# The first three steps of a second attention, moved into the tail of the dense programs before it

## The chip, the cores and the metric

The kernel runs on one NeuronCore of a Trainium2 chip. A core has five instruction queues that run side by side and meet only at semaphores: PE (matrix products, written to PSUM), ACT (ScalarE, functions of one tile), DVE (VectorE, elementwise work and sums), POOL (GpSimd) and SP (which starts DMAs). PSUM has eight banks of 512 float32 for each of 128 partitions; SBUF is the working memory. The metric is the device time of one execution in microseconds (us), the median of several runs.

## What is computed

Four blocks follow each other on a tensor x of 16 sequences x 256 tokens x 128 channels, each added to its input and normalised:

```python
x = layernorm(x + L0_attention(x))   # bucketed attention and a dense MLP
x = layernorm(x + L0_ffn(x))         # 8 experts on every token, gates from a global k-th value
x = layernorm(x + L1_attention(x))   # 4 local heads (softmax), 12 causal linear heads
x = layernorm(x + L1_ffn(x))         # 8 experts, top 2 of each token
```

The third line is the second attention. For each sequence (a block of 256 tokens) it needs x turned (channels on partitions), projections to q, k and v, a softmax over a causal window of 128 for four heads, and for the twelve others softmaxed queries against running sums of keys and values.

## The kernel before

The program has three stages, each with its own instruction block: `attention_0`, `dense_0` and `attention_1` (which also holds the routed experts at its end). Between two blocks every engine waits for every other, and the semaphores of the stage are cleared. Each stage allocates its own PSUM banks and SBUF tiles and gives them back.

`dense_0` runs 72 jobs (`JOBS`): 8 chunks of 512 tokens through the MLP, then 64 pairs of chunk and expert. A job is four hidden products into the banks `HB` (line 1097 to 1099), a gelu and a rounded copy on ACT (890, 895), a rest on DVE (936), and a down product into one of two banks `YB`. DVE then folds YB into the sum of the chunk (993, 1004): a down product waits until the fold of two jobs before has read its YB bank. `hidden` runs two jobs ahead (`LEAD`), so that the last two jobs issue down products alone and ACT has nothing left to do. When the last pair of a chunk is folded, PE turns the sum into the bank `PB` (1129), DVE adds the residual (`r`, 1055), takes mean and variance (1059, 1063), POOL raises the variance to -1/2 (876, 877), and DVE writes the normalised chunk to `keep["xa"]` (1085). Chunks end in the order 3, 0, 4, 5, 1, 6, 2, 7: chunk 2 at step `CLOSING` (69), chunk 7 at step 73, where the loop is otherwise empty. Up to 22 pairs are kept raw until the gates are known, 16 of them in `x1` and `xs`, the places of the first attention's results; the last of these 16 is folded at step 58.

`attention_1` works on 16 blocks of 256 tokens in a pipeline written out by hand. `PARTS_1` lists, for each step, which part of which block every engine issues; `parts_1` walks steps 0 to 16 and then `DRAIN_1`. Every engine walks the same list and issues only what is its own. The parts that matter here: `lift` (PE turns x into `BA`, 2124; ACT copies it to `xT`, 1874), `project` (PE, 2128, 2129; ACT rounds into `high`, 1879, 1880), `bias` (POOL adds a bias to x in place, 1822), `low` (DVE, 1958), `wide` (PE, 2134, into `BC` and `BD`), `heads` (DVE, 1966, 1971), `features` (ACT, 1896 to 1904, with the exponential), `keys` and `queries` (DVE, 1977, 1984, 1985), `scores` (PE into `SS`, 2156 to 2161), `max` (DVE, 1989, 1990), `context` (PE, 2144 to 2147; DVE divides, 2011 to 2015), `pad`, `qT`, `shift`. Step 0 has lift 0 alone; step 1 the projections and features of block 0 and lift 1; step 2 scores, max and context of block 0, projections and features of block 1, and lift 2. `wide` of a block waits for the division of the block before it, which reads the bank it overwrites.

`fetch` and `split` carry the routed experts' weights: SP brings a share of each matrix in, ACT scales it and rounds it (1935, 1938), POOL forms the rest (1827). Share n comes in step n + 1, two places in a ring. Before its steps, POOL of `attention_1` clears tiles (1801 to 1814).

The step list, cut to what is quoted above:

```python
PARTS_1 = [
    [("scores", 2), ("max", 2), ("project", 1), ("context", 2), ("pad", 2), ("back", 4), ("qT", 2), ("fetch", 1), ("bias", 1)],
    [("weights", 3), ("offset", 5), ("low", 1), ("wide", 1), ("heads", 1), ("shift", 2), ...
     ("features", 1)],
    [("values", 3), ("linear", 3), ("keys", 1), ("queries", 1), ("lift", 0), ("copy", 3), ... ("split", 1)]]
```

## Time and profile before

| | us |
|---|---|
| median of 3 runs | 1030.87 |
| their range | 1030.49 to 1030.97 |
| the profiled execution | 1030.6 |
| its span, first to last instruction | 1028.9 |
| PE busy | 933.9 (91%) |
| DVE busy | 817.0 (79%) |
| ACT busy | 780.1 (76%) |
| POOL busy | 433.2 (42%) |

The span is what lies between the first and the last recorded instruction; 1.7 us of the profiled execution lie around it. A busy time counts an engine's instructions, not its waits. A share of 91% over the whole span says little of a stage of 30 us, so that the stage is read by itself below. The granted clock (PEclk) is 1.00 at 2.4 GHz and 0.50 at 1.2 GHz.

### The profile page before, as it was taken

How to read it: one execution, taken by the hardware profiler on the slowest of the kernel's cores; microseconds unless marked ns; L12 is line 12 of the kernel's file. 1: busy time of each engine (PE TensorE's matmuls, PEld its weight loads, DVE VectorE, ACT ScalarE, POOL GpSimd, SP SyncE). 2: the span in 40 equal slices, each digit the busy share in tenths (PEclk: the TensorE clock that was granted, in tenths of full speed). 3: DMA queues.
4: the chain of work that ended last, by engine and by line, in shares of the span. 5: the costliest groups of instructions: out<-in, count | busy, mean ns of one | idle time of the engine just before them, and what ended most of it. 6: DMA issues, size and time to landing. Idle time of an engine off the chain costs nothing. (4 is left out here: it accounts for less than half of the span.)

```text
span 1028.9 us, 29035 instructions
## 1 busy us (share of the span) xinstructions
PE 933.9 (91%) x10222; PEld 603.1 (59%) x10222; DVE 817.0 (79%) x2282; ACT 780.1 (76%) x1537; POOL 433.2 (42%) x613
## 2 busy tenths in 40 slices
PE   5999999988999999999999999488888865899995
PEld 3788888874555444444444444256565644789862
DVE  4898888853777999688899899578888867888845
ACT  3789998977998888888888788166776643788844
POOL 3667777762352000000100100224687777666653
PEclk9999999987999999999999999789999975999998
DMA  8433333101000000222123221110111103232327
GB/s 273 146 127 126 130 128 127 46 23 33 1 1 1 1 1 1 77 83 80 55 81 88 67 82 52 34 32 22 41 57 49 49 25 82 78 87 82 82 59 213
DMA packets 61005, 72.60 MB, mean 71 GB/s; under 512 B 8875, under 2 KB 37805, under 8 KB 60865
## 3 DMA queue, kind: packets, MB, share of 16 engines
q1 hardware_dynamic: 50080, 59.36, 18.9%
q0 software_dynamic: 4544, 8.60, 2.5%
q10 hardware_dynamic: 6240, 2.79, 1.1%
q8 instruction: 86, 1.41, 0.6%
q14 instruction: 55, 0.44, 0.1%
HBM read 40.14 MB, written 31.49 MB: 70 GB/s over the span
## 5 line engine op out<-in xcount | busy, mean ns | idle before, releaser
L890 ACT ACTIVATE d__hf<-d__HB,dense__d 128x512 f32<-128x512 f32 x288 | 185.6, 680 | 48.4 <-PE d__HB L1099 47.4
L936 DVE TENSOR_TENSOR d__hl<-d__hf,d__hh 128x1024 f16<-128x1024 f32 x144 | 174.2, 1220 | 28.3 <-ACT d__hh L895 26.0
L876 POOL TENSOR_SCALAR d__rstd<-d__mv 128x4 f32<-128x4 f32 x16 | 14.2, 887 | 338.1 <-DVE d__mv L1063 338.1
L895 ACT ACTIVATE d__hh<-d__hf 128x1024 f16<-128x1024 f32 x144 | 152.2, 1057 | 4.6
L1097 PE MATMUL d__HB<-dense__xh,dense__w1h 128*128 128x512 f16 x288 | 110.0, 382 | 2.8 <-ACT d__hf L890 1.5
L1097 PE MATMUL d__YB<-d__hh,dense__w2h 128*128 128x512 f16 x288 | 109.2, 379 | 2.5 <-DVE d__tmp L993 2.5
L1098 PE MATMUL d__HB<-dense__xl,dense__w1h 128*128 128x512 f16 x288 | 110.1, 382 | 0.0
L1099 PE MATMUL d__HB<-dense__xh,dense__w1l 128*128 128x512 f16 x288 | 109.9, 382 | 0.0
L1098 PE MATMUL d__YB<-d__hl,dense__w2h 128*128 128x512 f16 x288 | 109.2, 379 | 0.0
L1099 PE MATMUL d__YB<-d__hh,dense__w2l 128*128 128x512 f16 x288 | 109.2, 379 | 0.0
L370 POOL TENSOR_SCALAR_AFFINE_SELECT a__pt<-a__pt 128x512 f32<-128x512 f32 x128 | 83.7, 676 | 56.6 <-ACT a__pt L418 56.6
L508 DVE TENSOR_REDUCE a__mx<-a__S 128x4 f32<-128x512 f32 x128 | 82.0, 683 | 20.6 <-PE a__S L612 20.4
L1358 POOL DMA_INDIRECT parts<-c__ys,c__dest x78 | 81.3, 1042 | 39.5 <-issue 17.6
L418 ACT ACTIVATE a__pt<-a__ST 128x512 f32<-128x512 f32 x128 | 69.4, 596 | 13.2 <-PE a__ST L628 13.1
L1844 POOL DMA_INDIRECT rows<-b__xr,b__slot x64 | 63.5, 992 | 21.5 <-issue 17.0
L1376 ACT ACTIVATE c__hf<-b__SS,c__bias 128x256 f32<-128x256 f32 x156 | 61.1, 474 | 7.5 <-PE b__SS L1585 6.8
L1512 DVE TENSOR_TENSOR c__hl<-c__hf,c__hh 128x512 f16<-128x512 f32 x78 | 54.2, 695 | 2.7
L1097 PEld LDWEIGHTS d__HB<-dense__xh,dense__w1h 128*128 128x128 f16 x288 | 30.4, 105 | 35.2 <-ACT d__hf L890 3.0
L1097 PEld LDWEIGHTS d__YB<-d__hh,dense__w2h 128*128 128x128 f16 x288 | 28.2, 98 | 36.0 <-DVE d__tmp L993 4.5
L1099 PEld LDWEIGHTS d__HB<-dense__xh,dense__w1l 128*128 128x128 f16 x288 | 28.3, 98 | 34.7 <-issue 1.1
L1099 PEld LDWEIGHTS d__YB<-d__hh,dense__w2l 128*128 128x128 f16 x288 | 28.2, 98 | 34.0
L1098 PEld LDWEIGHTS d__YB<-d__hl,dense__w2h 128*128 128x128 f16 x288 | 28.2, 98 | 31.8
(413 smaller groups left out, 2547.3 us busy)
## 6 DMA issues: line engine op xcount, KB each, us to landing
rows<-a__blank SPq DMA_DIRECT2D x72, 268.0 KB, 3.0
d__G<-gates SPq DMA_DIRECT2D x64, 256.0 KB, 3.2
c__xin<-rows SPq DMA_DIRECT2D x39, 134.0 KB, 2.2
dense__stage<-e_w SPq DMA_DIRECT2D x16, 256.0 KB, 3.2
b__stage<-e_w SPq DMA_DIRECT2D x32, 128.0 KB, 2.3
c__yb<-parts SPq DMA_DIRECT2D x8, 256.0 KB, 8.1
c__yb<-parts ACTq DMA_DIRECT2D x8, 256.0 KB, 8.8
out<-c__xo SPq DMA_DIRECT2D x8, 256.0 KB, 2.5
```

The source lines that it names most:

```text
L370: pool.affine_select(out=v, in_=v, compare_op=ALU.is_ge, fill=0.0, base=BK, pattern=[[0, 8], [1, BK]], channel_multiplier=-1).then_inc(cau ...
L418: act.activation(pt[:, u % 4, :], ST[:, u % 2, :], ACT.Exp, scale=scale).then_inc(exp_done, 1)
L508: dve.tensor_reduce(mx[:, u // 4, :, u % 4], S[:, u % 2, :].rearrange("p (a j) -> p a j", a=4), AX.X, ALU.max).then_inc(s_free, 1)
L890: act.activation(hf[:, q, f], HB[:, f], gelu, scale=1.0 / WS, bias=b1[:, at:at + 1]).then_inc(s_["h_free"], 1)
L895: act.activation(hh[:, j % (LEAD + 1), f - 1:f + 1], hf[:, q, f - 1:f + 1], ACT.Copy).then_inc(s_["hi_done"], 1)
L936: dve.tensor_tensor(hl[:, p, f], hf[:, q, f], hh[:, p, f], ALU.subtract).then_inc(s_["lo%d_done" % i], 1)
L1097: pe.matmul(dst, wh, vh, start=begin, stop=False)
L1098: pe.matmul(dst, wh, vl, start=False, stop=False)
L1099: return pe.matmul(dst, wl, vh, start=False, stop=end)
L1358: pool.indirect_dma_start(parts, bass.IndirectOffsetOnAxis(dest[b % RING][:, a:a + 1], 0), ys[b % RING][:, a, :], None, bounds_check=2 * T ...
L1376: ins = act.activation(hf[b % 2][:, f], HB[:, b % 2, f // 2, f % 2], ACT.Gelu, scale=1.0 / WS, bias=bias[:, f, b:b + 1])
L1844: pool.indirect_dma_start(rows, bass.IndirectOffsetOnAxis(slot[n % SENT][:, k, a:a + 1], 0), words[n % SENT][:, a, :], None, bounds_check= ...
```

## The change

The first three steps of `attention_1` (`EARLY_1`, 25 parts: lift 0, then block 0's projections and features, then block 0's scores and context and block 1's projections and features, up to lift 2) are issued from inside `dense_0`'s block. To make that possible the eight PSUM banks become one tensor `keep["banks"]` that both stages cut up (the attention's `BA` to `BD` are the banks of `HB`, its `SS` those of `YB`, `PB` and `QB`), and the attention's tiles come from `keep["lease"]`, the place of `x1` and `xs`. `attention_1` becomes a generator: it first hands out its early parts, and after the dense block it goes on with `MAIN_1`.

Where the early parts stand in each queue: PE issues lift 0 after the down product of the last job but one, project 0 and wide 0 after the last one, lift 1 after the last chunk is turned, and the rest (from scores 0) once the last read of PB is done. DVE issues low 0 and heads 0 at step `CLOSING` after the last folds and ahead of the normalised write of chunk 2; keys 0 and queries 0 between the variance of chunk 7 and its normalised write; the rest after that. ACT goes through its early parts after its loop, behind a first exponential on a scrap tile. POOL clears the tiles at step 66, after the raw pairs are folded, and adds the biases of blocks 0 and 1 after its last rstd. `fetch` and `split` stay behind: shares 0 and 1 both come in step 3, 2 and 3 both in step 4, then one in each step as before. The dense loop ends one empty step earlier.

```diff
+                if s == CLOSING - 3:
+                    pool.wait_ge(s_["g_used"], place[LAST_RAW] + 1)
+                    second["clears"](pool)
...
+            pool.wait_ge(keep["att_in"], 16 * 5)
+            in_order(EARLY_1, second["gpsimd"](pool))
...
+            act.wait_ge(keep["att_in"], 16 * 5)
+            second["warm"](act)
+            in_order(EARLY_1, second["scalar"](act))
...
                 if s == CLOSING:
                     fold(s + 1)
                     fold(s + 2)
+                    dve.wait_ge(keep["att_in"], 16 * 5)
+                    in_order(EARLY_1[:OPEN_1], attention)
...
+                if s == END - 1:
+                    in_order(EARLY_1[OPEN_1:LOOK_1], attention)
                 if post:
                     c = post[1]
...
+            in_order(EARLY_1[LOOK_1:], attention)
...
                 if 0 <= s < JOBS:
                     down(s)
+                if s == JOBS - 2:
+                    pe.wait_ge(s_["h_free"], 4 * JOBS)
+                    pe.wait_ge(keep["att_in"], 16 * 5)
+                    in_order(EARLY_1[:1], attention)
+                if s == JOBS - 1:
+                    in_order(EARLY_1[1:OPEN_1], attention)
...
+            in_order(EARLY_1[OPEN_1:LOOK_1], attention)
+            for q in range(2):
+                pe.wait_ge(s_["yf%d" % q], JOBS // 2)
+            pe.wait_ge(s_["pb_free"], len(left))
+            in_order(EARLY_1[LOOK_1:], attention)
...
+EARLY_STEPS = 3
+SPLITS_1 = {EARLY_STEPS: (0, 1), EARLY_STEPS + 1: (2, 3)}
...
+EARLY_1 = [u for s in range(EARLY_STEPS) for u in steps_1(s)]
+MAIN_1 = [u for s in range(EARLY_STEPS, NB + 1) for u in steps_1(s)] + DRAIN_1
+
+OPEN_1 = EARLY_1.index(("heads", 0)) + 1
+LOOK_1 = EARLY_1.index(("lift", 1)) + 1
...
+        def warmed(act):
+            act.wait_ge(s["cleared"], CLEARED_VALUES)
+            act.activation(scrap[:], half[:], ACT.Exp).then_inc(s["warm"], 1)
```

## Rows read from the trace of the kernel before

**Rows 1.** Chain that ended last, 660 to 690 us: start, length, engine, tile, line
```profile
...
666.00 1.28 ACT L1902
...
673.21 1.44 PE b__BC L2134 x2
...
681.89 0.81 PE b__BC L2134 x2
...
```

**Rows 2.** Busy time of single microseconds: engines (PE first), PEclk, DMA share, GB/s
```profile
...
652.00:653.00 1.00, 0.56 (x4) 0.32 (x4) 0.93 (x4) 0.00 (x0) 0.00 (x0) 0.80 0.00 0
...
666.00:667.00 1.00, 0.43 (x3) 0.01 (x1) 0.00 (x0) 1.00 (x1) 0.00 (x0) 0.88 0.00 0
...
676.00:677.00 1.00, 1.00 (x14) 0.45 (x12) 0.79 (x5) 0.44 (x4) 0.00 (x0) 0.76 0.00 0
...
```

**Rows 3.** Timeline of the dense tail: start, length, engine, line, tile, idle before and releaser
```profile
...
645.75 0.39 PE L1097 MATMUL d__YB<-d__hh,dense__w2h 128*128 128x512 f16 x1 [1.13 <-DVE d__tmp L993]
...
651.82 1.11 DVE L1085 TENSOR_SCALAR keep__xa<-d__r,d__mv,d__rstd 128x128 f32<-128x128 f32 x4
...
651.93 0.63 PE L1129 MATMUL d__PB<-keep__ident,d__acc 128*128 128x128 f32 x4 [3.42 <-DVE d__acc L1004]
653.04 0.69 DVE L1055 TENSOR_TENSOR d__r<-d__PB,keep__xa 128x512 f32<-128x512 f32 x1
...
656.67 1.11 DVE L1085 TENSOR_SCALAR keep__xa<-d__r,d__mv,d__rstd 128x128 f32<-128x128 f32 x4 [1.51 <-POOL d__rstd L877]
...
```

**Rows 4.** Timeline of the second attention's first steps, same columns
```profile
...
659.24 0.66 PE L2124 MATMUL b__BA<-keep__ident,keep__xa 128*128 128x128 f32 x2 [6.68 <-PEq L100]
...
660.00 0.38 ACT L1874 ACTIVATE b__xT<-b__BA 128x256 f32<-128x256 f32 x1 [19.28 <-PE b__BA L2124]
...
660.44 1.22 PE L2128 MATMUL b__BA<-b__xT,keep__b 128*128 128x256 f32 x2 [0.54 <-ACT b__xT L1874]
...
662.31 1.27 PE L2134 MATMUL b__BC<-keep__b,b__xT 128*128 128x320 f32 x2
...
663.41 0.48 DVE L1958 SCALAR_TENSOR_TENSOR b__qs<-b__high,keep__b,b__BA 128x256 f16<-128x256 f16 x1 [5.62 <-ACT b__high L1880]
...
665.01 0.41 PE L2156 MATMUL b__SS<-b__ks,b__qs 32*128 32x256 f16 x4
...
665.46 0.98 PE L2161 MATMUL b__SS<-keep__bbf 128*128 128x256 bf16 x4
...
669.78 0.64 PE L2144 MATMUL b__BC<-b__gv,b__kf 64*96 64x97 f32 x2
...
671.99 0.16 DVE L2011 TENSOR_SCALAR b__den<-b__BC 96x3 f32<-96x3 f32 x1 [1.16 <-PE b__BC L2147]
...
675.75 0.26 DVE L1966 TENSOR_REDUCE b__qm<-b__BC 128x12 f32<-128x96 f32 x1 [1.51 <-PE b__BD L2134]
...
678.32 0.70 PE L2128 MATMUL b__BA<-b__xT,keep__b 128*128 128x256 f32 x2 [1.07 <-ACT b__xT L1874]
...
678.71 1.16 DVE L1989 TENSOR_REDUCE b__mx<-b__SS 128x4 f32<-128x1024 f32 x1
...
680.67 0.16 DVE L2011 TENSOR_SCALAR b__den<-b__BC 96x3 f32<-96x3 f32 x1 [0.20 <-PE b__BC L2147]
...
683.27 0.26 DVE L1966 TENSOR_REDUCE b__qm<-b__BC 128x12 f32<-128x96 f32 x1 [0.35 <-PE b__BD L2134]
...
```

**Rows 5.** Timeline of POOL, then DVE, at one place of the dense programs
```profile
...
314.65 1.15 POOL L871 TENSOR_TENSOR dense__xl<-d__xT,dense__xh 128x512 f16<-128x512 f32 x1
...
314.71 1.94 DVE L1085 TENSOR_SCALAR keep__xa<-d__r,d__mv,d__rstd 128x128 f32<-128x128 f32 x4 [0.80 <-POOL d__rstd L877]
...
```

**Rows 6.** Timeline of ScalarE where step 3 passes into step 4
```profile
...
685.89 0.69 ACT L1935 ACTIVATE b__stage<-b__stage 128x512 f32<-128x512 f32 x1
...
688.12 0.38 ACT L1879 ACTIVATE b__high<-b__BA 128x256 f16<-128x256 f32 x1 [0.79 <-PE b__BA L2129]
...
689.89 0.38 ACT L1884 ACTIVATE b__qT<-b__BD 96x256 f32<-96x256 f32 x1 [1.02 <-PE b__BD L2140]
...
```

More of the change, by code:

```diff
@@ L1674, in blocks_1, with attention_1 @@
     return early, sync, gpsimd, scalar, vector, tensor, scalar_early, vector_early, tensor_early
-def attention_1(nc, d, keep, rows, parts, out, w1, w2, whole):
+def attention_1(nc, d, keep, rows, parts, out, w1, w2, whole, weights):
     with ExitStack() as ctx:
@@ new lines, in attention_1 @@
+        den = lease.sb([GW, 3])
+        rinv = lease.sb([GW, 3])
+        ctxn = [lease.sb([GW, 4, GW]) for p in range(2)]
+        mx = lease.sb([P, 2, LH])
+        mpad = lease.sb([P, 2, LH, 32], F16)
+        q2 = lease.sb([P, 2, P], F16)
+        pt = lease.sb([P, LH, 3 * P])
+        ots = lease.sb([P, 2 * P])
+        rc = lease.sb([P, 2, LH])
+        ob = lease.sb([P, 2, C])
+        aT = lease.sb([P, TB])
+        half = lease.sb([P, 2])
+        r = lease.sb([P, 2, C])
+        st = lease.sb([P, 2, 6])
@@ L1755, in attention_1 @@
+        mv = lease.sb([P, 2, 2])
+        rstd = lease.sb([P, 2])
+        mean_off = lease.sb([P, 2])
+        x3T = lease.sb([P, TB])
+        SS = banks[:, 4:8]
+        BA, BB, BC, BD = (banks[:, i] for i in range(4))
         OT, LN = SS[:, 0, 0:2 * P], SS[:, 1, 0:2 * GW]
@@ L1766, in attention_1 @@
         s = {n: m.sem(n) for n in names.split()}
-        for p in range(SENT):
-            s["sent%d" % p] = m.sem("sent%d" % p)
+        s.update((n, None) for n in later.split())
         def row_free(eng, q):
             wait(eng, s["sent%d" % (q % SENT)], q // SENT * 128)
-        keep["ident16"] = ident16
-        (early, sync, gpsimd, scalar, vector, tensor, scalar_early, vector_early,
-         tensor_early) = blocks_1(nc, Mem(nc, ctx, "c", whole), d, keep, rows, parts, out, (SS, BA, BB, BC, BD), s)
         scale = float(HD) ** -0.5
@@ L2245, in step @@
                     ins.then_inc(s["join_full"], 1)
-            parts_1(step)
+            return step
+        yield {"clears": clears, "warm": warmed, "gpsimd": gpsimd_steps, "scalar": scalar_steps,
+               "vector": vector_steps, "tensor": tensor_steps}
+        weights()
+        for n in later.split():
+            s[n] = m.sem(n)
+        for p in range(SENT):
+            s["sent%d" % p] = m.sem("sent%d" % p)
+        G = keep["G"]
+        lg = m.sb("lg", [P, 4, E])
+        lm = m.sb("lm", [P, 4])
@@ new lines, in attention_1 @@
+        slot = [m.sb(f"slot{p}", [P, 2, 4], U32) for p in range(SENT)]
+        words = [m.sb(f"xr{p}", [P, 4, ROW]) for p in range(SENT)]
+        xr = [v[:].rearrange("p a c -> p (a c)").bitcast(F16).rearrange("p (a c) -> p a c", a=4) for v in words]
+        tok, kval, earlier, ones = f32["tok"], f32["kval"], bf16["earlier"], bf16["ones"]
+        base = keep["base"]
+        share = w1.shape[1] // NB
+        stage = m.sb("stage", [P, 2, 2, share])
+        split_to = ((w1, keep["w1h"], keep["w1l"]), (w2, keep["w2h"], keep["w2l"]))
@@ new lines, in attention_1, with share_of @@
+        parts_of = share // P
+        def share_of(w, n):
+            e, f = n * parts_of // FB, n * parts_of % FB
+            return w[:, f:f + parts_of, e * P:(e + 1) * P]
+        keep["ident16"] = ident16
+        (early, sync, gpsimd, scalar, vector, tensor, scalar_early, vector_early,
+         tensor_early) = blocks_1(nc, Mem(nc, ctx, "c", whole), d, keep, rows, parts, out, (SS, BA, BB, BC, BD), s)
+        hooks.update(scalar=scalar_early, vector=vector_early, tensor=tensor_early)
+        block = ctx.enter_context(nc.Block())
@@ new lines, in _, with step @@
+        @block.sync
+        def _(sp):
+            early(sp)
+            def step(what, n):
+                if what == "fetch":
+                    wait(sp, s["split_low"], n - 1)
+                    for a, (src, _, _) in enumerate(split_to):
+                        sp.dma_start(stage[:, n % 2, a],
+                                     src[:, n * share:(n + 1) * share]).then_inc(s["landed%d" % (n % 2)], 16)
+            in_order(MAIN_1, step)
+            sync(sp)
+        @block.gpsimd
@@ new lines, in _ @@
+        def _(pool):
+            for w in words:
+                pool.memset(w[:, :, C + 5], 0.0)
+            pool.memset(chosen[:, 4], 0.0).then_inc(s["cleared"], 1)
+            pool.wait_ge(s["cleared"], CLEARED_ALL)
+            in_order(MAIN_1, gpsimd_steps(pool))
+            gpsimd(pool)
+        @block.scalar
+        def _(act):
+            in_order(MAIN_1, scalar_steps(act))
+            scalar(act)
+        @block.vector
+        def _(dve):
+            in_order(MAIN_1, vector_steps(dve))
+            vector(dve)
@@ L2269, in program, with routed_weights @@
         keep["fetch_att"] = fetch_att
+        c2 = ctx.enter_context(ExitStack())
+        def routed_weights():
+            m2 = Mem(nc, c2, "routed", m)
+            for n in ("w1h", "w1l", "w2h", "w2l"):
+                keep[n] = m2.sb(n, [P, FB, E * P], F16)
+            keep["G"] = m2.sb("G", [P, NT, E])
+        second = attention_1(nc, d, keep, rows, parts, out, d["e1_w1"], d["e1_w2"], m, routed_weights)
+        early = next(second)
         with ExitStack() as c1:
```

251 lines of the change are left out of this document (109 added, 142 removed).

## The prediction

> **What bounds the kernel now.** I read the page's 40 slices first. PE is busy nine tenths nearly everywhere, but at the border between the dense programs and the second attention all engines thin out and PEclk falls. So the next views were the timeline of that border, the chain that ended last, and the busy time of single microseconds.
>
> The tail of the dense programs is a chain on DVE. PE's last down product is over 3.42 us before PE turns the last sum at 651.93; in that time DVE folds the last pairs, then it writes chunk 2, takes the statistics of chunk 7 (653.04), waits 1.51 us for POOL's rstd and writes chunk 7 until 657.78 [rows 3]. PE and ACT have next to nothing to do there: PE also stands 1.13 us before the last down product [rows 3], and ACT idles 19.28 us before the attention's first copy [rows 4].
>
> Then the barrier between the blocks: PE's first transpose starts at 659.24, 1.46 us after the last write [rows 3, 4]. From there the chain runs hand to hand. Block 0 has no other block beside it: turn, copy, project, round, wide, heads, features (with an exponential table load of 1.28 us in the chain), context, divide, wide of block 1, and so on [rows 1, 4]. PE runs most of it at 1.2 GHz: the clock drops in the microsecond 652, after PE has stood for most of the 3.42 us, comes back only in 666, has gone again by the time PE does wide 1, and is back for good in 676 [rows 2]. The same wide product takes 2.54 us at 1.2 GHz (673.21 to 675.75, where DVE begins to read) and 1.38 us at 2.4 GHz (681.89 to 683.27) [rows 1, 4]. I take as the mark of comparison the division of block 1's context on DVE at 680.67 [rows 4]: from there on each part is the same work in both kernels, and the chain continues to the end, so a shift at this mark is a shift of the end. From the end of the dense write (657.78) to this mark the old kernel takes 22.89 us.
>
> **The change, part by part.**
>
> Beside the tail, at no cost. Lift 0 takes 0.66 us even at 1.2 GHz [rows 4] and lies in PE's 1.13 us gap. Project 0 and wide 0 come after the last down product: 1.87 us (660.44 to 662.31) and 2.54 us at 1.2 GHz, 4.41 together [rows 1, 4]; at 2.4 GHz, which PE has there, I estimate half of the first and 1.38 of the second, 2.3. They begin near 648.5 and are over near 650.8, inside the 3.42 us. If that cover fails they end at 652.9, the last sum is turned 1 us later, and DVE, which by then has other work until 655.0, still does not wait. The table load and the clears stand in queues that are empty (ACT's 19.28 us; POOL waits for the last rstd), so that features 0 no longer contain the 1.28 us. Were the load still in the way, it would cost at most that. The clears write SBUF beside dense steps in which PE sets the pace: nothing, or some tenths on a DVE that has room.
>
> On the path, delaying the dense tail. DVE is a queue in order: low 0 (two instructions of 0.48) and heads 0 (four of 0.26) stand ahead of chunk 2's write, with chunk 7's statistics, POOL's rstd and chunk 7's write queued behind: 2.00 us [rows 4]. Keys 0 and queries 0 are four instructions of about 0.3 us and lie in the 1.51 us of waiting for rstd: nothing, at worst their own 1.2 us in part. The bias of blocks 0 and 1 on POOL now starts when rstd is done, just when DVE writes chunk 7. The nearest row is a place where a POOL tensor_tensor ran beside the same DVE write: 1.94 us in place of 1.11 [rows 3, 5]. I take these 0.83 us once; the bounds are nothing and twice that. The Trainium skill ("SBUF — State Buffer", section "Who interferes with whom") says that DVE and GpSimd share a port pair as an exclusive lock, and that the loser waits for the whole instruction; the row agrees. Without this the forecast would be 0.83 lower.
>
> After the dense write, until the early steps end. Max 0 takes 1.76 us (678.71 to 680.67 less 0.20 of waiting), and its scores are ready, as PE needs only DVE's last read of PB, some 4 us earlier. The division until wide can start takes 1.22 (680.67 to 681.89). Wide 1 takes 1.38 or 2.54; I take 1.38, since scores 0, project 1 and context 0 keep PE at work just before. From DVE's first read of wide 1 to the end of queries 1 it is 2.96 (675.75 to 678.71) [rows 1, 4].
>
> The barrier, now here: 1.46 us again, as the same block ends and the same semaphores are cleared. It also empties the pipeline. In the old kernel scores 1 and project 2 ran beside step 2's end; now PE issues them after the barrier, with context 1 behind, before the mark is reached: at 1.2 GHz scores 1.43 (665.01 to 666.44), project 1.87, context 2.21 (669.78 to 671.99), together 5.51. At 2.4 GHz project and context take 2.35 (678.32 to 680.67), and with an estimated half for scores 3.07 [rows 4]. Before the barrier PE stands for some 3 us while DVE finishes, and it stood about as long before the drop in 652 [rows 2, 3], so I take 5.51. The Trainium skill ("TensorE: Matmul & The Clock Gate", section "HAM oscillation — how this bites in real kernels") says that a wait between bursts makes PE start cold each time; the trace agrees (1.2 GHz after each of its two waits here), and this rule speaks against the change, which puts a wait there. If the clock held, the time would be 2.44 lower.
>
> The doubled splits. Two shares less in steps 1 and 2, where ACT waited anyway; one more in each of steps 3 and 4, 1.44 us on ACT (685.89 to 687.33). Behind it stands the rounding for the next block, before which ACT idles 0.79 us, and then qT, before which it idles 1.02 [rows 6]: 1.81 us of cover against 1.44, so nothing. If the first gap alone counts, it is 0.65 in each step, 1.30 in all. The fetches go out earlier than ACT needs them by the length of a step.
>
> Sum from 657.78: 2.00 + 0.83 + 1.76 + 1.22 + 1.38 + 2.96 + 1.46 + 5.51 = 17.12, so the mark is reached at 674.90 in place of 680.67: 5.77 us earlier. The profiled execution (1030.6, of which 1028.9 are span) becomes 1024.8; the median of the runs lies 0.27 above the profiled execution, so I forecast 1025.1.
>
> **The rivals.**
>
> The clock holds over the barrier. PE then refills in 3.07, and with no collision on the ports the gain is 5.77 + 2.44 + 0.83 = 9.04: 1021.8. For it: PE has more to do than in the old tail. Against: the trace shows the drop after a wait of this size [rows 2, 3].
>
> Half of the gain is lost. Wide 1 at 1.2 GHz (1.16), the second bias (0.83) and the splits on the path (1.30) together take 3.29: gain 2.48, 1028.4. Each of the three has a row that allows it, but they are not bound to come together.
>
> No change. The moved steps don't run where they are put: DVE waits in low 0 or heads 0 for PE or ACT, and the tail waits behind it. Each microsecond of that wait is one of the end; 5.8 us are needed, so heads 0 would have to start near 658.5 in place of 652.8. Against: the inputs are ready by 651 by the sum above. 1030.9.
>
> Slower: the clock stays at 1.2 GHz beyond the refill. Each further step in the cold costs 1.16 for wide, 1.73 for project and context (4.08 against 2.35) and about 0.7 for scores, 3.6 us [rows 1, 4]. It decides from the second such step on: two cost 7.2 against the 5.77 won, 1032.3. For it: the old kernel lost the clock twice in these steps. Against: both times it came back within some 7 us of PE's resuming [rows 2, 4], and the fourth step has more for PE than the second.
>
> **How the numbers follow.** The forecast has 0.55 (its own range 1023.5 to 1026.7), the held clock 0.14, the half gain 0.16, no change 0.09, slower 0.06. The range from 1021.8 to 1028.4 leaves out the last two and the outer edges of the others. A difference under 0.2%, 2 us, can hardly be told from no change by a measurement of this kernel. Faster by more: 0.55 + 0.14 + 0.16 = 0.85; same 0.09; slower 0.06.
>
> **What would show it.** Right: lift 0 before the last down product; the table load near 641; low 0 at 651.8 and chunk 2's write at 653.8; chunk 7's write ending near 660.6, its instructions stretched beside the bias; no 1.28 us load inside features 0; the barrier over near 669.4; PEclk 0.50 in scores 1 and project 2; the division of block 1's context near 674.9, and each later step earlier by the same amount. Wrong: DVE idle ahead of low 0 or heads 0; a gap in front of max 0; a refill at 2.4 GHz; ACT's split as the releaser of the rounding's readers; or an end that moves by another amount than the mark, which would mean that a later stage gives back or adds.

## The result and the profile after

The kernel after the change takes 1023.55 us (median of 4 runs, 1022.05 to 1024.88); the kernel before, on the same chip, 1030.68 (1030.41 to 1030.97). The ratio is 0.993, with a 95% interval of 0.9913 to 0.9948. The profiled execution of after took 1024.88, of which 1023.2 are span; that of before 1030.6 and 1028.9. So the gain is 7.1 us by the medians and 5.7 between the two profiled executions.

Three moments carry all that follows. **Fold's end** is the end of the last fold in the dense tail on DVE (651.78 before: the sum that PE turns at 651.93 [rows 3]). **Division 1** is the mark of the prediction, the division of block 1's context on DVE. **Keys 2** is DVE's reciprocal for block 2, a later mark that also serves for kernels which move more or less than this one. Distances from the fold's end can be compared between executions; absolute times cannot, as the run called "again" below shows.

The timeline of after, ACT around 641, then PE and DVE from lift 0 on (start, length, engine, line, operation, tile out<-in; in brackets the idle time before and what ended it):

```profile
641.61 1.28 ACT L1832 ACT_TABLE_LOAD   x1
...
645.48 0.38 PE L2132 MATMUL keep__banks<-keep__ident,keep__xa 128*128 128x128 f32 x2
...
646.77 0.39 PE L1131 MATMUL keep__banks<-d__hh,dense__w2h 128*128 128x512 f16 x1 [0.91 <-DVE d__tmp L1022]
...
650.24 1.24 PE L2142 MATMUL keep__banks<-keep__b,keep__lease 128*128 128x320 f32 x4
...
652.12 0.69 DVE L1033 TENSOR_TENSOR d__acc<-d__acc,d__tmp 128x512 f32<-128x512 f32 x1
652.85 0.87 DVE L1969 SCALAR_TENSOR_TENSOR keep__lease<-keep__lease,keep__b,keep__banks 128x256 f16<-128x256 f16 x2
652.96 0.63 PE L1163 MATMUL keep__banks<-keep__ident,d__acc 128*128 128x128 f32 x4 [1.48 <-DVE d__acc L1033]
...
654.42 1.10 DVE L1118 TENSOR_SCALAR keep__xa<-d__r,d__mv,d__rstd 128x128 f32<-128x128 f32 x4
...
656.58 0.41 PE L2164 MATMUL keep__banks<-keep__lease 32*128 32x256 f16 x4 [2.37 <-DVE d__r L1084]
```

Here the covered part of the move is to be seen. The table load stands at 641.61, lift 0 just ahead of the last down product, and wide 0 is over by 651.5 beside the folds. Before, these steps began at 659.24, and scores 0 behind them only at 665.01 [rows 4]. Low 0 stands right behind the last fold, at 652.85, and chunk 2's write follows at 654.42.

The same timeline further on, POOL, DVE and PE up to division 1:

```profile
659.20 1.68 POOL L1839 TENSOR_TENSOR keep__xa<-keep__xa,keep__bo 128x128 f32<-128x128 f32 x4
659.26 1.70 DVE L1118 TENSOR_SCALAR keep__xa<-d__r,d__mv,d__rstd 128x128 f32<-128x128 f32 x4 [0.61 <-POOL d__rstd L900]
...
662.62 0.14 DVE L2022 TENSOR_SCALAR keep__lease<-keep__banks 96x3 f32<-96x3 f32 x1
...
663.82 2.50 PE L2142 MATMUL keep__banks<-keep__b,keep__lease 128*128 128x320 f32 x4 [2.37 <-DVE keep__lease L2026]
...
666.36 0.42 DVE L1977 TENSOR_REDUCE keep__lease<-keep__banks 128x12 f32<-128x96 f32 x2 [1.51 <-PE keep__banks L2142]
...
669.10 0.30 DVE L1996 RECIPROCAL keep__lease<-keep__lease 128x24 f32<-128x24 f32 x1
670.85 0.41 PE L2164 MATMUL keep__banks<-keep__lease 32*128 32x256 f16 x4 [3.89 <-PEq L100]
...
675.15 0.16 DVE L2022 TENSOR_SCALAR keep__lease<-keep__banks 96x3 f32<-96x3 f32 x1 [0.96 <-PE keep__banks L2155]
```

And the busy time of single microseconds of after (PE first; PEclk is the first figure behind the engines' brackets, then DMA share and GB/s):

```profile
658.00:659.00 1.00, 1.00 (x4) 0.82 (x3) 0.62 (x3) 0.00 (x0) 0.92 (x2) 0.50 0.00 0
...
662.00:663.00 1.00, 0.00 (x0) 0.00 (x0) 0.94 (x4) 0.00 (x0) 0.00 (x0) 1.00 0.00 0
...
664.00:665.00 1.00, 1.00 (x2) 0.66 (x3) 0.85 (x3) 0.00 (x0) 0.00 (x0) 0.50 0.00 0
...
671.00:672.00 1.00, 1.00 (x12) 0.52 (x5) 0.00 (x0) 0.00 (x0) 0.91 (x4) 0.50 0.11 25
...
674.00:675.00 1.00, 1.00 (x8) 0.76 (x8) 0.19 (x1) 0.72 (x2) 0.00 (x0) 1.00 0.67 194
```

The clock falls three times between 656 and 674, each time in a wait of PE or at its end (waits of 2.37, 2.37 and 3.89 us, ahead of 656.58, 663.82 and 670.85), and comes back each time after some 3 us of work. Wide 1 lies in the second low (2.50 us). So the stage that the change shortened is still one in which PE runs much of its work at 1.2 GHz.

From the fold's end (652.81) to division 1 (675.15) it is 22.34 us; before it was 28.89 (651.78 to 680.67 [rows 4]). That is 6.55 won. The next divisions stand at 683.79, 692.77 and 702.70, against 689.30, 697.98 and 707.91: 5.51, 5.21 and 5.21 us earlier, hardly less than the 5.52 at the mark. The fold's end itself came 1.03 later, so that 5.5 are left of the 6.55; 0.2 more come out in the rest of the kernel, and 5.7 is the difference of the spans.

The 1.03 have two parts. POOL's rstd for chunk 6 comes 0.73 later (621.49 against 620.76); 0.67 of it is there already 38 us after the start, and it lies within what executions of one kernel differ by (see "again"). The rest, 0.30, is new, and lies in the dense tail itself:

```profile
623.53 0.81 POOL L1819 MEMSET keep__lease<- 128x256 f32 x3
623.58 1.41 DVE L1118 TENSOR_SCALAR keep__xa<-d__r,d__mv,d__rstd 128x128 f32<-128x128 f32 x4 [1.18 <-POOL d__rstd L900]
...
624.78 0.92 POOL L1827 MEMSET keep__lease<- 96x384 f32 x2
624.91 0.68 DVE L1019 TENSOR_TENSOR d__tmp<-dense__stage,d__G 128x512 f32<-128x512 f32 x1
```

These are POOL and DVE of after at chunk 6's normalised write: it takes 1.41 us beside POOL's clears. In the kernel before the same write stood alone:

```profile
622.85 1.11 DVE L1085 TENSOR_SCALAR keep__xa<-d__r,d__mv,d__rstd 128x128 f32<-128x128 f32 x4 [1.18 <-POOL d__rstd L877]
```

### The profile page after: what moved, and what is told of

It reads as the page before. It is cut to its first block and busy times, and to the rows that moved or that the text cites. A ratio compares the mean times of both kernels' runs of the same rounds, so it can differ in the third digit from the quotient of the medians.

```text
span 1023.2 us, 29039 instructions
## 1 busy us (share of the span) xinstructions
PE 932.2 (91%) x10222; PEld 602.8 (59%) x10222; DVE 818.4 (80%) x2282; ACT 779.9 (76%) x1538; POOL 433.3 (42%) x613
## 3 DMA queue, kind: packets, MB, share of 16 engines
q8 instruction: 86, 1.41, 0.6%
## 5 line engine op out<-in xcount | busy, mean ns | idle before, releaser
L915 ACT ACTIVATE d__hf<-keep__banks,dense__d 128x512 f32<-128x512 f32 x288 | 185.5, 680 | 48.5 <-PE keep__banks L1133 47.5
L1131 PE MATMUL keep__banks<-dense__xh,dense__w1h 128*128 128x512 f16 x288 | 110.1, 382 | 2.8 <-ACT d__hf L915 1.5
L1131 PE MATMUL keep__banks<-d__hh,dense__w2h 128*128 128x512 f16 x288 | 109.2, 379 | 2.4 <-DVE d__tmp L1022 2.4
L1132 PE MATMUL keep__banks<-dense__xl,dense__w1h 128*128 128x512 f16 x288 | 110.0, 382 | 0.0
L1133 PE MATMUL keep__banks<-dense__xh,dense__w1l 128*128 128x512 f16 x288 | 109.9, 382 | 0.0
L1132 PE MATMUL keep__banks<-d__hl,dense__w2h 128*128 128x512 f16 x288 | 109.2, 379 | 0.0
L1133 PE MATMUL keep__banks<-d__hh,dense__w2l 128*128 128x512 f16 x288 | 109.2, 379 | 0.0
L528 DVE TENSOR_REDUCE a__mx<-keep__banks 128x4 f32<-128x512 f32 x128 | 82.0, 682 | 20.8 <-PE keep__banks L632 20.5
L438 ACT ACTIVATE a__pt<-keep__banks 128x512 f32<-128x512 f32 x128 | 69.4, 596 | 13.2 <-PE keep__banks L648 13.1
L1440 ACT ACTIVATE c__hf<-keep__banks,c__bias 128x256 f32<-128x256 f32 x156 | 61.1, 474 | 7.5 <-PE keep__banks L1649 6.5
```

The costliest lines, as they stand in the source:

```text
L528: dve.tensor_reduce(mx[:, u // 4, :, u % 4], S[:, u % 2, :].rearrange("p (a j) -> p a j", a=4), AX.X, ALU.max).then_inc(s_free, 1)
L915: act.activation(hf[:, q, f], HB[:, f], gelu, scale=1.0 / WS, bias=b1[:, at:at + 1]).then_inc(s_["h_free"], 1)
L1131: pe.matmul(dst, wh, vh, start=begin, stop=False)
L1132: pe.matmul(dst, wh, vl, start=False, stop=False)
L1133: return pe.matmul(dst, wl, vh, start=False, stop=end)
```

## The experiments

Each run is compared by distances from its own fold's end. "Rest of the span" is the span less the time of the fold's end, all that comes after it. The ratio is to the kernel before, timed beside each run; the experiments come from three chips, so medians of different rows compare best through their ratios.

| kernel | division 1 | keys 2 | rest of the span | median us | ratio, 95% interval |
|---|---|---|---|---|---|
| before | 28.89 | 34.23 | 377.1 | 1030.68 | |
| after | 22.34 | 27.69 | 370.4 | 1023.55 | 0.9930 [0.9913, 0.9948] |
| again | 22.56 | 27.91 | 370.4 | 1023.95 | 0.9950 [0.9934, 0.9966] |
| late_bias | 21.78 | 27.13 | 370.2 | 1022.71 | 0.9938 [0.9917, 0.9958] |
| no_warm | 22.41 | 27.76 | 369.9 | 1023.45 | 0.9937 [0.9906, 0.9968] |
| two_steps | 25.09 | 31.74 | 373.6 | 1026.53 | 0.9961 [0.9944, 0.9979] |
| filled | 19.89 | 25.24 | 368.4 | 1020.21 | 0.9919 [0.9898, 0.9939] |
| two_steps_filled | 19.90 | 25.29 | 367.0 | 1019.86 | 0.9917 [0.9894, 0.9940] |
| paced_clears | 22.44 | 27.79 | 369.5 | 1021.41 | 0.9928 [0.9909, 0.9946] |
| more_early | 17.50 | 26.54 | 368.9 | 1022.38 | 0.9938 [0.9920, 0.9956] |
| before_filled | 26.74 | 32.08 | 373.3 | 1027.85 | 0.9988 [0.9975, 1.0001] |
| two_best | 19.62 | 25.02 | 366.7 | 1019.38 | 0.9901 [0.9879, 0.9923] |
| three_best | 16.44 | 25.97 | 368.2 | 1020.56 | 0.9911 [0.9891, 0.9932] |
| three_mid | 16.46 | 26.68 | 369.6 | 1020.66 | 0.9920 [0.9900, 0.9940] |

The kernel before gave medians of 1028.7 to 1030.7 beside these runs. In more_early, three_best and three_mid, division 1 stands ahead of the barrier; there only keys 2 compares.

**again.** The kernel after the change, unaltered, to see what differs between executions of one kernel.

> The changed kernel once more, for a second trace of it. The executions seen so far lie between 1022.05 and 1024.88 us, and the one with a trace is the slowest. Theory: the spread comes from the TensorE clock in the moved steps, which stands at 1.2 or 2.4 GHz for wide 1 (2.54 or 1.38 us) and for the products behind the barrier (4.30 us in the first trace, 3.1 at 2.4 GHz); then the stretch from the last fold of the dense programs to the division of block 1's context, 22.34 us in the first trace (28.89 before), differs here by 1 to 2 us and the time with it. Rival: the spread comes from the start, where the first transpose waited 0.72 us longer for a load than in the trace of before; then the stretch stays within 0.2 of 22.34 and the dense programs begin earlier or later.

The stretch to division 1 is 22.56 against 22.34, and the rest of the span is the same, 370.4. So the theory is out and the rival holds, though not at the load that it names: what happens behind the fold's end repeats within some tenths; what varies is when the fold ends. Over the executions profiled, POOL's fourth rstd in the first attention comes between 35.4 and 38.3 us, though PE starts within 1.2 us of the same time. Two of them, after and then the run called filled:

```profile
38.19 0.19 POOL L348 TENSOR_SCALAR a__rstd<-a__mv 128x2 f32<-128x2 f32 x1
```

```profile
35.44 0.20 POOL L348 TENSOR_SCALAR a__rstd<-a__mv 128x2 f32<-128x2 f32 x1
```

That scatter, 2.9 us in all, arises long before the part of the program that the change moves. Most of it comes in one stretch: from the second rstd to the third it is 11.6 to 11.9 us in seven of the fourteen traces (11.64 in filled) and 13.4 to 13.7 in the other seven (13.56 in after, 13.60 in before). The scatter is as large as most effects looked for here, which is why the readings below rest on distances. What decides between the two lengths stays open.

**late_bias.** POOL adds the biases of blocks 0 and 1 behind the barrier, and no longer beside chunk 7's write.

```diff
-            in_order(EARLY_1, second["gpsimd"](pool))
...
-            in_order(MAIN_1, gpsimd_steps(pool))
+            pool.wait_ge(keep["att_in"], 16 * 5)
+            in_order([("bias", 0), ("bias", 1)] + MAIN_1, gpsimd_steps(pool))
```

> POOL adds the biases of blocks 0 and 1 after the barrier instead of beside the write of the last dense chunk. Theory: the write goes back from 1.70 us to 1.11 and all behind it comes 0.6 earlier, so the stretch from the last fold to the division of block 1's context is 0.6 shorter at the same clock; time about 0.6 lower. Rival: the write was stretched by something else (an instruction fetch, the turn into PSUM); then it stays at 1.7 and nothing moves.

DVE's row for chunk 7's write:

```profile
656.35 1.11 DVE L1116 TENSOR_SCALAR keep__xa<-d__r,d__mv,d__rstd 128x128 f32<-128x128 f32 x4 [0.62 <-POOL d__rstd L900]
```

1.11 in place of 1.70, and division 0 stands 0.59 earlier (9.22 against 9.81 behind the fold's end). The theory holds: the collision is real, and it costs 0.59. At division 1 and keys 2 0.56 of it is left; at the end of the span only 0.2, a size that the rest of the kernel scatters by anyway.

**no_warm.** The table load is not moved: features 0 load the exponential themselves.

```diff
-            second["warm"](act)
```

> The exponential on the scrap tile is left out, so that its table of 1.28 us is loaded inside features 0. Theory: features 0 then end 1.28 later, near 657.1, but DVE comes to keys 0 only at 657.7, and PE to project 1 at 657.9; so the load stays hidden and the time is the same within 0.3 us. Rival: the load is again in the chain, as it was in the kernel before, and the end comes 1.0 to 1.3 later.

Division 1 at 22.41, keys 2 at 27.76: nothing lost, as the theory had it. The load stands inside features 0, and the path does not see it:

```profile
652.68 1.28 ACT L1915 ACT_TABLE_LOAD   x1
653.98 0.28 ACT L1915 ACTIVATE keep__lease<-keep__lease 128x96 f32<-128x96 f32 x1
```

DVE is busy with chunk 2's and chunk 7's parts until it reads the features. The moved load is a part of the change that does nothing; what took it off the path is that features 0 now run beside the dense tail.

**two_steps.** Two steps moved in place of three; block 0's scores and context and all of block 1 stay behind the barrier.

```diff
-EARLY_STEPS = 3
-SPLITS_1 = {EARLY_STEPS: (0, 1), EARLY_STEPS + 1: (2, 3)}
+EARLY_STEPS = 2
+SPLITS_1 = {EARLY_STEPS: (0, 1)}
```

> Only the first two steps are moved (up to lift 1); step 2 runs behind the barrier, shares 0 and 1 of the weights both in step 2. Theory: the barrier is over near 662.2 (dense write near 660.7), the division of block 0's context comes 4.3 later at 666.5, and from there the trace of before had 8.68 us to the division of block 1's context, without a barrier between: near 675.2, the same as with three steps (675.15), because the third step wins only what the refill of the pipeline behind the barrier costs it. Time within 1 us of the changed kernel. Rival: each moved step is worth its share of the gain, so that without the third about a third to a half of the 7 us is lost, 2.5 to 3.5 us slower than the changed kernel.

Division 1 comes at 25.09, 2.75 later than with three steps, and the median is 3.0 us above that of after and 2.6 above that of again, which was timed beside it. The theory's "same as with three steps" is out and the size is the rival's, but not for the rival's reason. The single microseconds of two_steps tell what happened:

```profile
655.00:656.00 1.00, 0.00 (x0) 0.00 (x0) 0.97 (x4) 0.37 (x2) 0.00 (x0) 1.00 0.00 0
...
657.00:658.00 1.00, 0.00 (x0) 0.00 (x0) 0.84 (x4) 0.00 (x0) 0.75 (x2) 0.50 0.00 0
...
676.00:677.00 1.00, 1.00 (x6) 0.67 (x4) 0.00 (x0) 0.12 (x1) 1.00 (x3) 0.50 0.29 78
...
681.00:682.00 1.00, 1.00 (x30) 0.78 (x30) 0.94 (x5) 0.17 (x2) 0.00 (x0) 1.00 0.00 0
```

PE stands for 7.90 us over dense tail and barrier. The clock falls in 656 and stays at 0.50 until 680, although PE works again from 661.33 and is full in most microseconds. This is the mechanism of the slower rival of the prediction, at work in a form of the change that moves less; that it is the whole loss, two_steps_filled shows. One of the ten executions took 1022.18 us and the others 1025.0 or more; only a slower one has a trace, so that it isn't shown whether the clock stays low as long in each.

**filled.** Sixty products without use in PE's waits of the early block, into a part of a bank that nobody reads then; nothing else is altered.

```diff
+for k, unit in enumerate((("lift", 1), ("qT", 0), ("lift", 2))):
+    EARLY_1.insert(EARLY_1.index(unit) + 1, ("fill", k))
...
+                if what == "fill":
+                    if n == 2:
+                        pe.wait_ge(s["q2_done"], 1)
+                    for _ in range((20, 24, 16)[n]):
+                        pe.matmul(BB[:, TB:2 * TB], identb[:], causal[:], start=True, stop=True)
```

> Sixty products of 128x256 without use are put into PE's waits of the early block (20 behind lift 1, 24 behind qT 0, 16 behind lift 2), into a part of BB that nobody reads then. Theory: wide 1 and the refill behind the barrier are slow only because PE stood before them and the clock fell to 1.2 GHz. With PE busy, wide 1 takes about 1.4 us in place of 2.50, scores 1, project 2 and context 1 about 3.1 in place of 4.3, and the stretch from the last fold's end to the division of block 1's context is 20.0 to 20.3 us in place of 22.3; the time is some 2.3 us under that of the kernel after the change. Rival: the clock falls in the barrier whatever PE does before it, or the fills stand in front of scores 0 and wide 1: the stretch stays at 22.3 or grows.

PE's rows of wide 1 and of the first product behind the barrier, then two single microseconds of the same kernel, ahead of wide 1 and at the refill:

```profile
660.49 1.34 PE L2149 MATMUL keep__banks<-keep__b,keep__lease 128*128 128x320 f32 x4 [1.34 <-DVE keep__lease L2028]
...
666.37 0.30 PE L2171 MATMUL keep__banks<-keep__lease 32*128 32x256 f16 x4 [1.45 <-PEq L100]
```

```profile
660.00:661.00 1.00, 0.51 (x2) 0.43 (x3) 0.97 (x5) 0.00 (x0) 0.00 (x0) 1.00 0.00 0
...
666.00:667.00 1.00, 0.63 (x12) 0.47 (x13) 0.00 (x0) 0.00 (x0) 0.59 (x6) 1.00 0.00 0
```

The clock stays at 1.00 from 645 to 680. Wide 1 takes 1.34 in place of 2.50, and from scores 1 to division 1 it is 2.98 (666.37 to 669.35) in place of 4.30: 1.16 + 1.32 = 2.48, and the stretch is 2.45 shorter. So what the fills win in the early block is the clock and nothing else.

**two_steps_filled.** The two-step form, with 56 such products behind lift 1, where PE stood.

> Two steps moved in place of three, and 56 products of 128x256 without use behind lift 1, where PE waits for the dense tail and the barrier. Theory: what the two-step form lost (its stretch from the last fold's end to the division of block 1's context is 25.1 us against 22.3 with three steps) is the clock, which stood at 1.2 GHz for 24 us. Kept busy, PE holds 2.4 GHz: scores 0 to context 0 about 2 us less, wide 1 1.2 less, project 2 and context 1 1.7 less, so that the stretch is about 20.2 and the time under that of the three-step form. Rival: the loss is the order of the parts (a pipeline that starts again behind the barrier), and the stretch stays at 24 or above.

```profile
652.64 6.28 PE L2132 MATMUL keep__banks<-keep__bbf 128*128 128x256 bf16 x56
660.72 0.30 PE L2170 MATMUL keep__banks<-keep__lease 32*128 32x256 f16 x4 [1.79 <-PEq L100]
```

PE's rows show one block of fills over the tail, then scores 0 behind the barrier, at full clock. Division 1 is reached at 19.90, 5.19 earlier than without the fills (the theory had about 20.2), and level with the three-step form (19.89). The two-step form has one bias in place of two beside chunk 7's write, which takes 1.40 us there and 1.71 in filled; so up to 0.3 us may hide in this equality. Beyond that, with the clock held it makes no difference whether the third step stands ahead of the barrier or behind it; the 2.75 us that its place earned in the change are the clock's.

**before_filled.** The kernel before, nothing moved, with fills behind the last down product, behind the last sum turned and ahead of project 1.

```diff
+                if s == JOBS - 1:
+                    pe.wait_ge(s_["h_free"], 4 * JOBS)
+                    for _ in range(9):
+                        pe.matmul(HB[:, 0], w1h[:, 0:P], xh[:, toks(0)], start=True, stop=True)
...
+            for _ in range(22):
+                pe.matmul(HB[:, 0], w1h[:, 0:P], xh[:, toks(0)], start=True, stop=True)
...
+                    if n == 1:
+                        for _ in range(20):
+                            pe.matmul(BB[:, TB:2 * TB], identb[:], causal[:], start=True, stop=True)
```

> The kernel before, nothing moved; only products without use in PE's waits: 9 of 128x512 behind the last down product, 22 behind the last sum turned, 20 of 128x256 ahead of project 1. It asks how much of the gain is to be had without the move. Theory: the first steps of the attention lose by the clock alone 0.9 us in project 0, 1.2 in wide 0, 1.0 in context 0 and 1.2 in wide 1; the stretch from the last fold's end to the division of block 1's context falls from 28.9 to some 24.7, so that the move itself is worth 4 to 5 us more when the clock holds in both (19.9 with the move and fills). Rival: the clock falls in the barrier and in ACT's table load whatever stands before them, and the stretch stays above 27.

The stretch falls by 2.15, about half of the 4.2 expected, and the time by 1.3 us (ratio 0.9988, an interval that just reaches 1). PE's first rows behind the barrier and the clock there:

```profile
658.23 0.55 PE L2130 MATMUL b__BA<-keep__ident,keep__xa 128*128 128x128 f32 x2 [1.93 <-PEq L100]
```

```profile
658.00:659.00 1.00, 0.55 (x2) 0.20 (x2) 0.00 (x0) 0.12 (x1) 0.81 (x4) 0.68 0.00 0
...
665.00:666.00 1.00, 1.00 (x10) 0.86 (x9) 0.00 (x0) 1.00 (x1) 0.00 (x0) 0.90 0.00 0
```

The fills hold the clock over the tail, but between the last fill and lift 0 PE stands for 1.93 us, and the clock falls in 658. Project 0 and wide 0 run at 1.2 GHz as before; it is back in 665. The rival was right for block 0, the theory for block 1. Of the 1.93 us 1.46 are the barrier; the fills ended 0.47 ahead of DVE's last write (656.30 and 656.77). A wait of 1.45 us at the barrier did not cost the clock in filled, so that a few more fills might have held it here too; this was not run. Between this form and filled lie 6.85 us (26.74 against 19.89). They hold the order of the work and the clock of block 0 together: project 0 and wide 0 take 4.21 us here (659.31 to 663.52) and 2.11 in after beside the tail (649.37 to 651.48). An estimate from these rows leaves some 4.7 us that belong to the order alone.

**paced_clears.** POOL's clears six steps earlier.

```diff
-                if s == CLOSING - 3:
+                if s == CLOSING - 9:
...
-                    pool.wait_ge(s_["g_used"], place[LAST_RAW] + 1)
+                    pool.wait_ge(s_["g_used"], place[CLOSING - 8] + 1)
```

> POOL's clears stand six steps earlier, so that they don't run beside the normalised write of chunk 6. Theory: POOL's memsets beside DVE's write stretched that write from 1.11 us to 1.41 and so delayed the whole tail; the write is back at 1.11 and the distance from chunk 6's rstd to the last fold's end is 0.3 us shorter. A gain of that size can only be seen in the stretch, hardly in the time. Rival: the 0.3 us have another source and the distance stays, or the clears stretch whatever DVE instruction they meet and the tail is as late as before.

POOL at its new place with DVE's fold and rest beside it, and the write of chunk 6:

```profile
605.01 0.81 POOL L1819 MEMSET keep__lease<- 128x256 f32 x3
```

```profile
605.01 0.69 DVE L1033 TENSOR_TENSOR d__acc<-d__acc,d__tmp 128x512 f32<-128x512 f32 x1
...
622.62 1.11 DVE L1118 TENSOR_SCALAR keep__xa<-d__r,d__mv,d__rstd 128x128 f32<-128x128 f32 x4 [1.19 <-POOL d__rstd L900]
```

The write is back at 1.11, and from chunk 6's rstd to the fold's end it is 31.04 us (620.52 to 651.56) in place of 31.32; before it was 31.02. At the new place the clears stand beside tensor_tensor instructions of DVE, and these keep their 0.69. So it is the pair that counts: the same memsets stretch one DVE instruction and leave another alone. The median is 2.1 us lower, but the ratio to the kernel before beside it is all but the same (0.9928 against 0.9930), and only these 0.28 can be put down to the clears.

**more_early.** Scores 1, max 1, context 1, project 2, pad 1 and qT 1 of the fourth step are issued ahead of the barrier too.

```diff
+MORE_1 = [("scores", 1), ("max", 1), ("context", 1), ("project", 2), ("pad", 1), ("qT", 1)]
+EARLY_1 = [u for s in range(EARLY_STEPS) for u in steps_1(s)] + MORE_1
+MAIN_1 = [u for s in range(EARLY_STEPS, NB + 1) for u in steps_1(s) if u not in MORE_1] + DRAIN_1
```

> Scores 1, max 1, context 1, project 2, pad 1 and qT 1 of the fourth step are issued ahead of the barrier too. Theory: the 4.3 us of refill behind the barrier come from the pipeline that is emptied there; if PE does these products while DVE finishes the keys and queries of block 1, only wide 2 stands behind the barrier, and it begins 1.6 to 2.0 us earlier behind the last fold's end than the 23.6 us of the kernel after the change (if it runs at 1.2 GHz there, 1.2 of these go again). Rival: the part ahead of the barrier grows by as much as the refill shrinks, as max 1 and the division of block 1 now stand on DVE before the barrier; wide 2 begins where it did, within 0.5 us.

PE's rows at the barrier:

```profile
670.15 0.37 PE L2189 MATMUL keep__banks<-keep__lease 32*128 32x128 f16 x12 [2.67 <-PEq L100]
...
670.91 1.70 PE L2143 MATMUL keep__banks<-keep__b,keep__lease 128*128 128x320 f32 x4
```

Wide 2 begins 21.33 us behind the fold's end (649.58), 2.2 earlier than in after (23.56), a little more than the theory's 1.6 to 2.0: the refill is indeed work that can stand ahead of the barrier. But PE stands for 2.67 us at the barrier, the clock falls during wide 2, and at keys 2 1.15 of it is left.

**two_best.** Two steps moved, with the 56 fills, the bias of block 0 behind the barrier and the clears earlier: the edits of two_steps_filled, late_bias and paced_clears together.

> Two steps moved, with the fills behind lift 1, the bias of block 0 behind the barrier and the clears six steps earlier. Theory: the parts add: 0.3 from the clears and 0.3 from chunk 7's write without a bias beside it come to the two-step form with fills (1019.9), which gives about 1019.3, stretch 19.6. Rival: the bias behind the barrier lies then in the way of the shares' POOL work, and nothing is won: 1019.9 or more.

1019.38 us, ratio 0.9901; keys 2 at 25.02 in place of 25.29. The time is where the theory put it (1019.3), but the 0.5 us between this and two_steps_filled are less than its interval. It is the best median of the study, under that of the kernel after by 4.2 us, and by 3.0 through the ratios (0.9901 against 0.9930).

**three_best.** Three steps and more_early's parts, with late_bias, paced_clears and fills (20 behind lift 1, 22 behind qT 0, 10 behind qT 1).

> Three steps and the fourth's scores, max, context and project moved, with fills behind lift 1, qT 0 and qT 1, both biases behind the barrier and the clears six steps earlier. Theory: what was won apart adds up: with the clock held, wide 2 begins 19.8 to 20.3 us behind the last fold's end (21.1 with fills alone, 21.3 with the longer early part alone), and the time is 1018.5 to 1019.5. Rival: with the clock held DVE is the bound of the early block, the longer early part wins nothing beyond the fills, wide 2 begins at about 21 and the time is that of the filled form, 1020.2, less 0.9 for the two small parts.

Wide 2 begins 21.90 us behind the fold's end (650.07), later than either theory or rival said. PE's rows, then the clock:

```profile
665.71 1.22 PE L2142 MATMUL keep__banks<-keep__lease,keep__b 128*128 128x256 f32 x2
...
668.00 1.64 PE L2132 MATMUL keep__banks<-keep__bbf 128*128 128x256 bf16 x10
...
671.97 1.24 PE L2148 MATMUL keep__banks<-keep__b,keep__lease 128*128 128x320 f32 x4
```

```profile
663.00:664.00 1.00, 0.01 (x1) 0.00 (x0) 0.10 (x1) 1.00 (x9) 0.00 (x0) 1.00 0.00 0
...
666.00:667.00 1.00, 1.00 (x3) 0.82 (x3) 0.93 (x5) 0.00 (x0) 0.00 (x0) 0.50 0.00 0
```

PE stood in 663 for features 1, the clock fell in 665, project 2 and the first of the last fills ran at 1.2 GHz, and the fills, over at 669.64, were by then the last thing ahead of the barrier; DVE's last instruction had ended at 667.99.

**three_mid.** The same, with the last ten fills behind scores 1 in place of qT 1.

> As the run with three steps and the fourth's first products moved and fills, but the ten last fills stand behind scores 1, where PE waited 1.4 us there and then lost the clock, and none stand behind qT 1, where they were the last thing ahead of the barrier. Theory: that run missed its numbers (wide 2 at 21.9 us behind the last fold's end) only by where its last fills stood; now project 2 takes about 1.0 us in place of 2.0, DVE ends the early block, and wide 2 begins 20.0 to 20.4 us behind the fold's end, the time about 1.5 us less. Rival: the wait ahead of the barrier takes the clock anyway or the barrier is bound by something other than PE's fills: wide 2 begins at 20.9 or later.

```profile
665.01 0.70 PE L2142 MATMUL keep__banks<-keep__lease,keep__b 128*128 128x256 f32 x2
...
669.03 0.53 PE L2194 MATMUL keep__banks<-keep__lease 32*128 32x128 f16 x12 [2.67 <-PEq L100]
...
670.32 2.34 PE L2148 MATMUL keep__banks<-keep__b,keep__lease 128*128 128x320 f32 x4
```

Now project 2 runs at 2.4 GHz and wide 2 begins at 20.82, 1.1 earlier than in three_best, but PE stands for 2.67 us ahead of it, the clock falls, and wide 2 takes 2.34: keys 2 comes at 26.68, later than in three_best. The rival was right about the clock: with nothing for PE in the last 2.67 us ahead of the barrier's end, it is lost. For wide 2 the result lies between the theory (20.0 to 20.4) and the rival (20.9 or later). Neither place of the fills brings keys 2 of the longer early part to that of filled (25.24); fills at both places were not tried.

## Why the prediction was right, and where it was not

The forecast was 1025.1 and the profiled execution to be 1024.8; it took 1024.88. The sum behind it held less well than this. From the end of the write of chunk 7 as it stood before (6.00 us behind the fold's end) to division 1 the prediction had 17.12 us; after has 16.34. Its terms, read from the rows of after:

| term | predicted | measured | from to |
|---|---|---|---|
| low 0 and heads 0 ahead of chunk 2's write | 2.00 | 1.57 | 652.85 to 654.42 |
| chunk 7's write beside the bias | 0.83 | 0.59 | 1.70 less 1.11 |
| max 0 | 1.76 | 1.66 | 660.96 to 662.62 |
| division until wide 1 starts | 1.22 | 1.20 | 662.62 to 663.82 |
| wide 1 | 1.38 | 2.54 | 663.82 to 666.36 |
| wide 1 to the end of queries 1 | 2.96 | 3.04 | 666.36 to 669.40 |
| barrier | 1.46 | 1.45 | 669.40 to 670.85 |
| refill | 5.51 | 4.30 | 670.85 to 675.15 |

Right, with its place: the covered lift 0, project 0 and wide 0; the barrier; the collision of the bias with chunk 7's write, which late_bias shows to be the bias's (the size was 0.24 too large; the row it came from has another POOL instruction beside the write [rows 5]); and the shift that stays with every later division but for 0.3 us.

These 0.3 are the doubled splits, put at nothing. From division 2 to division 3 it is 8.98 us (683.79 to 692.77) in place of 8.68: ACT goes from the last split of step 3 (682.70) into the rounding (683.00) without a gap. All forms with three steps have 8.97 to 9.03 there, and the forms with two, which double no split at that place, 8.68 or 8.69 as before. The second doubled split costs nothing (9.93 to the next division in both kernels).

The collision is smaller than the prediction's sentence on the shared ports would make it. In after POOL's four additions take 1.68 us, no more for each than the two that run at 671.13 with no write beside them (0.86), and the write beside them grows by 0.59 alone: for the most part the two ran side by side, and the write did not wait out each of POOL's instructions.

Wide 1 was the step that failed. "I take 1.38, since scores 0, project 1 and context 0 keep PE at work just before": PE stood for 2.37 us ahead of it, during max 0 and the division, and the clock fell there. In filled, with the clock at 1.00 ahead of it, the same product takes 1.34; the clock made it 2.50. The prediction had this price as one end and took the other.

The refill was 1.21 too dear for the opposite reason. Its scores and project ran at 1.2 GHz as said; the clock was back in 674 and context ran at full speed. These two errors cancel within 0.05, which is luck. The rest of the agreement is chance too: the stretch came out 0.78 shorter than the sum, and the fold's end 1.03 later than before, 0.73 of it by the scatter of the start. By the median of the runs, which leans less on one start, the time is 1.5 us below the forecast and just inside its own range.

Low 0 and heads 0 were 0.43 too dear: 2.00 was taken from the sum of single durations (0.48 and 0.26 each), while in a row of six the starts lie closer together. Durations of back-to-back instructions on DVE overlap in the trace; the time between the first and the next start is the price.

The clears were "nothing, or some tenths on a DVE that has room". It was 0.30, and DVE had no room: chunk 6's write is part of the chain of folds that sets the tail. Paced_clears shows both the cause and the price.

The table load was placed at nothing, and no_warm shows that it was worth nothing moved or not, because of what else was moved.

The prediction set against the slower rival that "both times it came back within some 7 us of PE's resuming". That is no property to rely on: in two_steps it took 19 us (661.33 to 680). For the change as made it did not come to this; two_steps beside it shows that the third step is what kept it from it. The held clock, forecast at 1021.8 with no collision, is what filled with its 1020.2 does (with the collision left in): the rival was sized about right, and the change alone does not reach it.

What stays open: behind keys 2 all these kernels do nearly the same work, and yet it takes between 341.3 us (before_filled) and 343.2 (filled) in the profiled executions. 0.3 of this are the doubled splits, which before, before_filled and the two-step forms don't have there. The rest has no cause found, and executions of one kernel differ by tenths too: from division 5 to 6 it is 11.11 us in after and 11.46 in again. So differences under 1 us between the filled forms are not settled.

## What to carry to other kernels

When work is moved into a thin stretch, count what the moved work does to TensorE's waits before counting its own time: here the third step was worth 2.75 us for keeping PE busy, and products without use in its place won all of that and more (5.19 us). A barrier empties the pipeline: put a price on each product that then stands behind it with nothing beside it, and look at what PE does in the microseconds ahead of it. And an engine pair can collide in one instruction and not in the next: put side work of POOL beside a DVE instruction that the trace shows unharmed.

## What the hardware showed

The granted clock stayed at 1.2 GHz under load in one of these kernels. In two_steps it was 0.50 from 657 to 680, with PE full in most microseconds from 662 on and its waits there at most 0.74 us; in after it came back some 3 us after each of three falls. The Trainium skill ("TensorE: Matmul & The Clock Gate", section "A second HAM failure mode: psum-queue depth-cycling") describes short idle times between groups of products that make the clock go back and forth; in two_steps it did not go back and forth but stayed low, and which of PE's short waits kept it there no run tells.

A wait of PE of nearly the same length cost the clock in one place and not in another: 1.38 us ahead of context 1 in three_best and 1.93 us at the barrier of before_filled lost it, 1.45 us at the barrier of filled and 1.79 us at that of two_steps_filled did not.

POOL's memsets, which only write SBUF, stretched DVE's tensor_scalar from 1.11 us to 1.41 and left tensor_tensor with two SBUF inputs at 0.69 and 0.68, the lengths that it has in the kernel before. The Trainium skill ("SBUF — State Buffer", section "Who interferes with whom") says that tensor_scalar can enter a mode that takes the shared port pair, and that an instruction with two SBUF inputs contends with a GpSimd instruction that reads SBUF and not with one that only writes; both halves agree with these rows.
